# Two steps of small products interleaved on TensorE, with orders chosen anew, in a seven-attention transformer kernel

## The chip, the cores and the metric

One core of a Trainium2 chip runs the whole program. The metric is the time of one execution on the device in microseconds (us), as the median of the runs. PE is TensorE, DVE VectorE, ACT ScalarE, POOL GpSimd and SP SyncE.

## The reference

Four samples of 256 tokens with 128 features go through four blocks: ten sublayers in all. Seven are attention with 16 heads of 8 features, three are MLPs of 512 hidden features. What is computed, cut down:

```python
# x [4, 256, 128], cond [4, 128], ctx [4, 256, 128]
def attend(q, k, v, kind):                     # 16 heads of 8 features
    s = einsum('bhqd,bhkd->bhqk', q, k) / sqrt(8)
    if kind == 'window': # only keys of the same 64 tokens, tokens rolled by 32
        ...
    if kind == 'topk':   # softmax over the 16 largest scores of each query only
        top_s, top_i = top_k(s, 16)
        ...
    return einsum('bhqk,bhkd->bhqd', softmax(s), v)

# block 0: full self-attention, full cross-attention to ln(ctx), MLP (gelu)
# block 1: full self-attention, full cross-attention to ctx, MLP (gelu)
# block 2: full cross-attention to a modulated ln(ctx)
# block 3: window self-attention, top-16 cross-attention to ctx, MLP (swiglu)
x = x + gate * (attend(q(ln(x)), k(src), v(src), kind) @ w_o + b_o)
x = x + gate * (act(ln(x) @ w_up + b_up) @ w_down + b_down)
```

Layer norms are modulated by shifts and scales made from silu(cond).

## The kernel before

The program is a list of steps for each engine. A step is a tuple (kind, b, l, u): a kind of work, a sample b (0 to 3), a sublayer l and a part u. `plan` (lines 623 to 917) makes the lists before the program is emitted. It simulates the five engines with a table of durations (`BUSY`, line 147), takes whatever is ready, and where several steps are, the one with the highest rank: the length of the work behind it plus `LEAD` (per sample and sublayer), `BIAS` (per engine and kind) and `EXTRA` (per engine, kind, sample and sublayer). These three tables of numbers set the orders. The plan also hands out PSUM's eight banks (ring "bank"), the slots of the exponentials' buffer and others, and the emitted program waits on semaphores for what the plan says had them before. So each engine runs its list strictly in the order written.

For a full attention of one sample the steps are: PE makes queries and keys ("qk", lines 1517 and 1518); ACT and POOL split them in parts; four DMAs of POOL's queue bring them to the buffer `QKS` ("stack", line 1158), where each of four planes s holds four groups g of 32 rows, one head pair's operands in each. "scores" u = 0 to 7 (line 1536) multiplies groups 2(u%2) and 2(u%2)+1 of plane u//2, for both halves t of the queries: four matmuls of 32 rows and 256 columns into two banks. DVE takes the maxima of each step (line 1406). PE transposes the maxima, ACT copies them and a DMA of SP's queue writes them into row 31 of each group ("maxima"). "weights" u = 0 to 7 (line 1566) is the transposed product in the same form, on the same groups of rows; ACT makes the exponential of it (line 1298). "mix" (line 1590) multiplies with the values, then come the division, the output projection and the addition to x.

The window attention does eight smaller matmuls in each of four scores steps, and four in each weights step. In the top-k attention a step "topk" u = 0 to 15 (line 1544) makes one head's scores on the one group u%4 into one bank; DVE finds and strikes out the 8 largest twice (lines 1416, 1419, 1426, 1429), POOL makes a mask of what is left (line 1227), and PE adds it to the weights by eight more matmuls (line 1577).

The planner knows that steps on different groups of rows overlap on PE: `groups` (line 815) gives a step's groups as bits, and `beside` (line 822) says that a step starts right behind one that shares no group with it. Such a step gets 10 more in its rank (`BESIDE`) and costs 0.22 us less (with 0.2 us until its result is there). Scores and full weights steps cost 0.46 us, topk steps 0.4 us. Where PE would be idle for over 0.3 us, the plan puts spare matmuls on the identity (`SPARE`, line 1473).

In the emitter for PE a step's matmuls stand together. For scores:

```python
for i, s in enumerate(planes_of_scores(l, u)):
    pe.wait_ge(stacked[b][s], 16 * (l + 1))
    for t in range(NT):
        ...
        for j in range(2):
            g = 2 * (u % 2) + j
            ins = nc.tensor.matmul(...)
ins.then_inc(fin, 1)
```

## Time and profile before

| | us |
|---|---|
| median of 3 runs | 670.6 |
| lowest and highest of them | 669.71 and 672.51 |
| the profiled execution | 665.29 |
| its span, first to last instruction | 663.5 |
| PE busy | 570.0 |
| DVE busy | 490.9 |
| ACT busy | 386.3 |
| POOL busy | 306.4 |

The mean granted clock of PE was 0.863 of its full speed. Busy times are unions over the span; matmuls are pipelined, and a matmul's length in the trace includes time in which the next ones already run, so what a step costs PE is read from the start of the next one. PEld is the load of a matmul's stationary operand. "idle before" and "<-" give the idle time of the engine ahead of an instruction, and what ended it. L1536 is line 1536 of the kernel.

### The profile page before, as it was taken

To read this page: it belongs to the slowest core of one execution; us is meant where nothing else is said; L and a number is where in the kernel's file an instruction comes from. 1 tells how busy PE (TensorE), PEld (TensorE's weight loads), DVE (VectorE), ACT (ScalarE), POOL (GpSimd) and SP (SyncE) were. 2 spreads that over 40 slices of the span, in tenths; PEclk is the share of its full clock that TensorE was granted. 3 is DMA by queue.
4 is the path that set the end of the run, shared out by engine and by line. 5 is a ranking of instruction groups with operands and counts; after the bars stand their busy time and mean duration, and the time that the engine had idled before them with its cause. 6 is when DMAs were issued, how large, how long until landed. Compare 5 with 4: busy or idle time off the path is not lost.

```text
span 663.5 us, 14489 instructions
## 1 busy us (share of the span) xinstructions
PE 570.0 (86%) x5152; PEld 378.9 (57%) x5152; DVE 490.9 (74%) x1291; ACT 386.3 (58%) x669; POOL 306.4 (46%) x584
## 2 busy tenths in 40 slices
PE   3888989899999999999998889786999987867477
PEld 3645556566756565657665556554655664634246
DVE  2577767853859687745377727999999999999953
ACT  2546878799696887886757766452233531611133
POOL 6884535435845444364562446641341446111133
PEclk9858999999999999998989979777575795765779
DMA  9560344302333533020335043140020002000000
GB/s 319 143 159 3 88 106 112 73 2 54 76 67 69 105 77 78 2 65 2 66 72 123 2 129 68 28 101 0 2 65 2 2 10 64 9 1 2 1 2 16
DMA packets 15062, 39.23 MB, mean 59 GB/s; under 512 B 2641, under 2 KB 6801, under 8 KB 14737
## 3 DMA queue, kind: packets, MB, share of 16 engines
q0 software_dynamic: 8960, 29.37, 20.1%
q1 hardware_dynamic: 5312, 8.46, 3.8%
q8 instruction: 43, 0.70, 0.4%
q10 hardware_dynamic: 720, 0.49, 0.3%
q14 instruction: 27, 0.21, 0.1%
HBM read 7.96 MB, written 0.52 MB: 13 GB/s over the span
## 4 chain that ended last, share of the span: by engine, by line
DVE 38%; PE 37%; ACT 8%; DMA 6%; issue 6%; POOL 4%; ACTq 0%; POOLq 0%
PE psum L1590 10%; DVE left L1419 8%; DVE left L1429 7%; DVE top L1426 6%; DVE top L1416 6%; DVE maxima L1406 5%; PE psum L1566 5%; PE psum L1536 5%; ACT softmax_T L1298 4%; DMA qk_stack<-centred 3%; PE psum L1625 3%; PE psum L1636 3%; DMA qk_stack<-qk_parts 2%; DVE maxima L1402 2%; PE psum L1617 2%
## 5 line engine op out<-in xcount | busy, mean ns | idle before, releaser
L1298 ACT ACTIVATE softmax_T<-psum 128x1024 f32<-128x1024 f32 (+1 forms) x224 | 210.9, 962 | 111.7 <-PE psum L1577 73.3
L1406 DVE TENSOR_REDUCE maxima<-psum 128x4 f32<-128x1024 f32 x160 | 190.1, 1216 | 52.4 <-PE psum L1536 51.6
L1566 PE MATMUL psum<-qk_stack 32*128 32x256 f32 (+1 forms) x896 | 114.9, 346 | 28.1 <-DMA qk_stack<-centred 9.6
L1590 PE MATMUL psum<-softmax_T,values 128*32 128x256 f32 (+1 forms) x1792 | 129.9, 408 | 4.8 <-ACT softmax_T L1298 3.5
L1566 PEld LDWEIGHTS psum<-qk_stack 32*128 32x128 f32 x896 | 72.3, 202 | 71.0 <-issue 31.0
L1227 POOL TENSOR_SCALAR unpicked<-left 128x512 bf16<-128x512 f32 x64 | 39.5, 616 | 136.0 <-DVE left L1429 135.3
L1536 PE MATMUL psum<-qk_stack 32*128 32x256 f32 (+1 forms) x768 | 89.6, 335 | 9.2 <-ACT softmax_T L1298 2.4
L1536 PEld LDWEIGHTS psum<-qk_stack 32*128 32x128 f32 x768 | 58.9, 200 | 37.5 <-issue 16.5
L1590 PEld LDWEIGHTS psum<-softmax_T,values 128*32 128x32 f32 x1792 | 56.7, 118 | 40.3 <-issue 12.0
L1187 POOL TENSOR_TENSOR qk_parts<-qk_parts 128x256 fp32r<-128x256 f32 x56 | 40.9, 730 | 77.0 <-ACT qk_parts L1281 76.6
L1158 POOL DMA_DIRECT2D qk_stack<-qk_parts x112 | 63.7, 580 | 7.0 <-POOL qk_parts L1187 6.3
L1306 ACT ACTIVATE centred<-psum 8x256 f32<-8x256 f32 (+1 forms) x64 | 23.1, 364 | 56.3 <-PE psum L1551 40.9
L1278 ACT ACTIVATE qk_parts<-psum,column_biases 128x512 fp32r<-128x512 f32 x56 | 38.5, 687 | 24.0 <-PE psum L1518 21.0
L1419 DVE MATCH_REPLACE8 left<-top,psum 128x256 f32<-128x256 f32 x128 | 52.0, 414 | 0.0
L1429 DVE MATCH_REPLACE8 left<-top,left 128x256 f32<-128x256 f32 x128 | 51.4, 408 | 0.0
L1416 DVE MAX8 top<-psum 128x8 f32<-128x256 f32 x128 | 48.1, 417 | 2.0 <-PE psum L1544 2.0
L1426 DVE MAX8 top<-left 128x8 f32<-128x256 f32 x128 | 47.9, 416 | 1.3
L1448 DVE TENSOR_TENSOR x<-x,psum 128x256 f32<-128x256 f32 x40 | 16.6, 414 | 41.2 <-PE psum L1636 22.9
L1473 PE MATMUL psum<-identity 128*128 128x256 bf16 x150 | 27.4, 332 | 19.4 <-DVE left L1419 11.5
L1310 ACT ACTIVATE mixed_T<-psum 128x256 f32<-128x256 f32 x56 | 21.5, 385 | 31.9 <-PE psum L1590 31.3
L1172 POOL TENSOR_SCALAR centred<-x,neg_mean,rstd 128x128 f32<-128x128 f32 x80 | 35.2, 447 | 4.4
L1168 POOL TENSOR_SCALAR neg_mean<-mean_var 128x2 f32<-128x2 f32 x48 | 9.4, 196 | 58.6 <-DVE mean_var L1394 44.1
(99 smaller groups left out, 870.3 us busy)
## 6 DMA issues: line engine op xcount, KB each, us to landing
qk_stack<-qk_parts POOLq DMA_DIRECT2D x112, 256.0 KB, 5.1
weights<-in_w SPq DMA_DIRECT2D x1, 1408.0 KB, 13.5
row_biases<-in_rows SPq DMA_DIRECT2D x1, 1088.0 KB, 10.8
weights<-in_w SPq DMA_DIRECT2D x2, 512.0 KB, 5.9
weights<-in_w SPq DMA_DIRECT2D x1, 832.0 KB, 9.0
qk_stack<-centred SPq DMA_DIRECT2D x48, 8.0 KB
weights<-in_w SPq DMA_DIRECT2D x1, 768.0 KB, 4.3
weights<-in_w SPq DMA_DIRECT2D x1, 576.0 KB, 3.7
```

Of the source, the lines that this page charges most:

```text
L1158: pool.dma_start(QKS[b][:, u, :, :].bitcast(F32), parts[32 * u:32 * u + 32, slot, :, :, :].bitcast(F32)).then_inc(stacked[b][u], 16)
L1187: nc.gpsimd.tensor_tensor(lo, lo.bitcast(F32), parts[:, slot, 0, c, :].bitcast(F32), ALU.subtract).then_inc(done[kind, "pool"], 1)
L1227: nc.gpsimd.tensor_scalar(unpicked[:, n, :, :], left[:, k, :, :], 1.0 / GONE, 1.0, ALU.mult, ALU.add).then_inc(done[kind, "pool"], 1)
L1298: nc.scalar.activation(pT[:, slot, u % 2, :, 0:cols].rearrange("p (i t) n -> p i t n", t=NT), two_banks(step).rearrange("p i (t n) -> p i ...
L1406: nc.vector.tensor_reduce(rows[:, u // 4, u // 2 % 2, g:g + 2, :], ps.rearrange("p i (t k) -> p i t k", t=NT), AX_X, ALU.max).then_inc(fin, 1)
L1416: ins = nc.vector.max(top8[:, b, r, g, t, :], misc[:, N * t:N * t + N])
L1419: ins = nc.vector.match_replace(left[:, k, t, :], top8[:, b, r, g, t, :], misc[:, N * t:N * t + N], -GONE)
L1426: ins = nc.vector.max(top8[:, b, 2, g, t, :], left[:, k, t, :])
L1429: ins = nc.vector.match_replace(left[:, k, t, :], top8[:, b, 2, g, t, :], left[:, k, t, :], -GONE)
L1536: ins = nc.tensor.matmul(ps[:, j, at:at + (P if window else N)], QKS[b][32 * g:32 * g + 32, s, 0, P * t:P * t + P], QKS[b][32 * g:32 * g + ...
L1566: ins = nc.tensor.matmul(ps[:, i, t, 0:P if window else N], QKS[b][32 * g:32 * g + 32, s, 1, P * t:P * t + P], QKS[b][32 * g:32 * g + 32, ...
L1590: ins = nc.tensor.matmul(misc[32 * g:32 * g + 32, queries], V[:, b, t, first:first + 32], pT[:, slot, g // 2, 2 * (g % 2) + t, 0:P if wind ...
```

## The change

1. A step "weaves" if it is a full attention's scores, a topk step, or the weights of a full or window attention. When `plan` takes such a step for PE, it looks among PE's ready steps for another that weaves, on no common group, that can start within `TOGETHER` = 0.15 us. It takes the one with the highest rank, unless a step that doesn't fit has a rank higher by more than `BESIDE`. The two are planned as one piece of 0.50 us (0.40 behind a step beside the first), with the results at 0.46 and 0.52 us.
2. The emitter for PE waits for the banks and inputs of both steps and then issues half 0 of the first, half 0 of the second, half 1 of the first, half 1 of the second. A weaving step without partner is emitted as before.
3. In the plan an odd scores or weights step of a full attention (weights also of the window) no longer depends on the even one ahead of it, and scores of the window depend on both their planes' stacks.
4. The plan charges 0.62 instead of 1.0 us for POOL's stack step.
5. All of `EXTRA`, `BIAS` and `LEAD` are other numbers, so the orders of all engines, the slots and the spare matmuls are others.

```diff
-    ("pe", "qk"): 1.0, ... ("pool", "stack"): 1.0,
+    ("pe", "qk"): 1.0, ... ("pool", "stack"): 0.62,
...
+WOVEN, WOVEN_BESIDE, WOVEN_FIRST, WOVEN_SECOND, WOVEN_SLOWER, TOGETHER = 0.5, 0.1, 0.46, 0.52, 1.5, 0.15
...
+def weaves(step):
+    kind, b, l, u = step
+    if kind == "topk":
+        return True
+    return kind == "scores" and ATTN[l]["kind"] == "full" or kind == "weights" and ATTN[l]["kind"] != "topk"
...
-                    pe = task("pe", ("scores", b, l, u), stack[planes_of_scores(l, u)[-1]], t and ("pe", ("scores", b, l, u - 1)))
+                    pe = task("pe", ("scores", b, l, u), *[stack[s] for s in planes_of_scores(l, u)],
+                              ("pe", ("scores", b, l, u - 1)) if u and (u % 2 == 0 or lay["kind"] == "window") else None)
...
-                t = task("pe", ("weights", b, l, u), maxed[u // 2], prev and ("pe", ("weights", b, l, u - 1)),
+                t = task("pe", ("weights", b, l, u), maxed[u // 2], ("pe", ("weights", b, l, u - 1)) if u and (u % 2 == 0 or topk) else None,
...
+        if eng == "pe" and weaves(step):
+            others = [(rank(n), c[0], n) for n in ready["pe"] if (c := choose(n)) is not None]
+            fit = [o for o in others if weaves(o[2][1]) and not groups(o[2]) & groups(t) and o[1] <= s + TOGETHER]
+            if fit:
+                r, at, other = max(fit, key=lambda o: o[0])
+                if any(r + BESIDE < o[0] for o in others if o not in fit and o[1] <= s + 0.3):
+                    other = None
...
+        if other is not None:
+            s = max(s, at)
+            d = WOVEN - (WOVEN_BESIDE if beside(t, s) else 0.0)
+            last = groups(other)
+            end = clock.run(s, d, cells(step) + cells(other[1]), WOVEN_SLOWER)
+            ready["pe"].remove(other)
+            hold(other, choose(other)[1])
+            free["pe"] = end
+            woven[step] = other[1]
...
+            def inputs_in(step):
+                kind, b, l, u = step
+                if kind == "weights":
+                    pe.wait_ge(max_in[b], maxima_count(l, u // 2 if ATTN[l]["kind"] == "topk" else u // 4))
+                elif kind == "topk":
+                    pe.wait_ge(stacked[b][u // 4], 16 * (l + 1))
+                else:
+                    pe.wait_ge(stacked[b][u // 2], 16 * (l + 1))
+
+            def half(step, t):
+                kind, b, l, u = step
+                if kind == "topk":
+                    s, g = u // 4, u % 4
+                    return nc.tensor.matmul(bank(step)[:, N * t:N * t + N], QKS[b][32 * g:32 * g + 32, s, 0, P * t:P * t + P],
+                                            QKS[b][32 * g:32 * g + 32, s, 1, :], start=True, stop=True)
+                s, ps = u // 2, two_banks(step)
+                own, other = (1, 0) if kind == "weights" else (0, 1)
+                moving = slice(P * t, P * t + P) if ATTN[l]["kind"] == "window" else slice(0, N)
+                for j in range(2):
+                    g = 2 * (u % 2) + j
+                    ins = nc.tensor.matmul(ps[:, j, t * N:t * N + moving.stop - moving.start],
+                                           QKS[b][32 * g:32 * g + 32, s, own, P * t:P * t + P],
+                                           QKS[b][32 * g:32 * g + 32, s, other, moving], start=True, stop=True)
+                return ins
...
+                if weaves(step):
+                    inputs_in(step)
+                    if step in WOVEN_WITH:
+                        other = WOVEN_WITH[step]
+                        banks_free(pe, other)
+                        inputs_in(other)
+                        half(step, 0)
+                        half(other, 0)
+                        half(step, 1).then_inc(fin, 1)
+                        half(other, 1).then_inc(done[other[0], "pe"], 1)
+                    else:
+                        half(step, 0)
+                        half(step, 1).then_inc(fin, 1)
...
-LEAD = [[29.6, 27.3, 159.8, 27.1, 27.2, 25.2, 30.7, 27.0, 78.1, 420.1],
-        [18.3, 18.3, 18.3, 19.7, 18.7, -13.4, -10.7, -63.6, 338.4, -332.4],
-        [9.3, 9.1, 50.8, 7.5, 8.8, 525.5, 13.5, -500.4, -1.8, 224.2],
-        [1.3, 1.4, 437.2, -0.3, 0.9, -1.2, 4.4, 87.9, 52.7, -9.6]]
+LEAD = [[26.4, 26.8, 28.3, 27.1, 26.9, 28.9, 27.5, 21.7, 82.5, 1258.6],
+        [18.1, 18.0, 18.8, 18.2, 18.3, 19.5, 19.5, 9.1, -55.3, 769.2],
+        [8.9, 9.0, 35.6, 9.0, 9.2, 8.6, 8.3, -12.9, 633.7, 830.7],
+        [0.2, 0.0, 1.3, -1.4, 2.8, 187.4, 2.4, -3.5, -53.3, 404.5]]
```

## Rows read from the trace of the kernel before

**Rows 1.** The page, busy time (us), share of the span and instructions of each engine.

```profile
PE 570.0 (86%) x5152; PEld 378.9 (57%) x5152; DVE 490.9 (74%) x1291; ACT 386.3 (58%) x669; POOL 306.4 (46%) x584
```

**Rows 2.** Stretches: start:end, length, then busy us (instructions) per engine, clock, DMA share, GB/s.

```profile
50.00:400.00 350.00, 326.66 (x3368) 214.17 (x3366) 230.03 (x370) 271.37 (x459) 174.16 (x338) 0.97 0.29 65
250.00:300.00 50.00, 48.24 (x505) 31.08 (x506) 30.85 (x54) 41.94 (x67) 23.10 (x42) 1.00 0.20 45
450.00:600.00 150.00, 121.90 (x844) 80.43 (x842) 145.43 (x543) 51.01 (x84) 49.00 (x86) 0.68 0.08 17
400.00:664.00 264.00, 209.13 (x1577) 140.56 (x1577) 234.90 (x862) 94.57 (x167) 92.42 (x165) 0.74 0.10 23
```

**Rows 3.** Groups of DVE from 405 to 640 us: count | busy us, mean ns | idle.

```profile
L1419 DVE MATCH_REPLACE8 left<-top,psum 128x256 f32<-128x256 f32 x128 | 52.0, 414 | 0.0
L1429 DVE MATCH_REPLACE8 left<-top,left 128x256 f32<-128x256 f32 x128 | 51.4, 408 | 0.0
L1416 DVE MAX8 top<-psum 128x8 f32<-128x256 f32 x128 | 48.1, 417 | 2.0 <-PE psum L1544 2.0
L1426 DVE MAX8 top<-left 128x8 f32<-128x256 f32 x128 | 47.9, 416 | 1.3
```

**Rows 4.** Timeline of DVE: first and last search pass, last addition (start us, length us).

```profile
411.01 0.76 DVE L1416 MAX8 top<-psum 128x8 f32<-128x256 f32 x2 [1.95 <-PE psum L1544]
...
636.40 0.41 DVE L1429 MATCH_REPLACE8 left<-top,left 128x256 f32<-128x256 f32 x1
...
660.81 0.42 DVE L1448 TENSOR_TENSOR x<-x,psum 128x256 f32<-128x256 f32 x1 [1.77 <-PE psum L1636]
```

**Rows 5.** Timeline of PE's matmuls from 240 to 243 us, some of them.

```profile
240.03 0.38 PE L1536 MATMUL psum<-qk_stack 32*128 32x256 f32 x2
240.04 0.39 PE L1566 MATMUL psum<-qk_stack 32*128 32x256 f32 x2
240.25 0.28 PE L1536 MATMUL psum<-qk_stack 32*128 32x256 f32 x2
240.26 0.28 PE L1566 MATMUL psum<-qk_stack 32*128 32x256 f32 x2
240.47 0.71 PE L1523 MATMUL psum<-weights,context_T 128*128 128x128 f32 x4
...
242.66 0.50 PE L1536 MATMUL psum<-qk_stack 32*128 32x256 f32 x4
243.09 0.38 PE L1617 MATMUL psum<-gated_projection,normed_T 128*128 128x128 f32 x1
```

**Rows 6.** Timeline of PE, first and last of the 99 adjacent pairs.

```profile
28.94 1.56 PE L1536 MATMUL psum<-qk_stack 32*128 32x256 f32 x10 [1.42 <-ACT context_T L1248]
...
383.45 0.51 PE L1566 MATMUL psum<-qk_stack 32*128 32x128 f32 x8
```

**Rows 7.** Timeline of PE, two pairs whose steps start apart.

```profile
119.68 0.50 PE L1566 MATMUL psum<-qk_stack 32*128 32x256 f32 x4
120.18 0.51 PE L1536 MATMUL psum<-qk_stack 32*128 32x256 f32 x4
...
257.82 0.38 PE L1536 MATMUL psum<-qk_stack 32*128 32x256 f32 x2
257.99 0.38 PE L1566 MATMUL psum<-qk_stack 32*128 32x256 f32 x2
258.05 0.28 PE L1536 MATMUL psum<-qk_stack 32*128 32x256 f32 x2
...
258.42 0.33 PE L1605 MATMUL psum<-identity,centred 128*128 128x128 f32 x1
```

**Rows 8.** Groups by shape over the span: exponential and maximum.

```profile
L1298 ACT ACTIVATE softmax_T<-psum 128x1024 f32<-128x1024 f32 x192 | 192.6, 1021 | 100.5 <-PE psum L1577 73.3 <-PE psum L1566 25.5
L1406 DVE TENSOR_REDUCE maxima<-psum 128x4 f32<-128x1024 f32 x160 | 190.1, 1216 | 52.4 <-PE psum L1536 51.6
```

**Rows 9.** Groups by shape over the span: POOL's issue of a stack.

```profile
L1158 POOL DMA_DIRECT2D qk_stack<-qk_parts x112 | 63.7, 580 | 7.0 <-POOL qk_parts L1187 6.3 <-issue 0.4
```

More of the change, by code:

```diff
@@ L782, in plan @@
     lists = {e: [] for e in engines}
-    clock, spare = Clock(), {}
+    clock, spare, woven = Clock(), {}, {}
     table, last, queue = "exp", 0, 16.0
@@ L871, in plan @@
         d, lag = busy(t), 0.0
+        since = max([free["pe"], IDENTITY_THERE] + [when for _, which in taken for when, _, _ in which])
+        hold(t, taken)
+        other = None
[5 more added lines that the diff above has]
+                if any(r + BESIDE < o[0] for o in others if o not in fit and o[1] <= s + 0.3):
+                    other = None
+        if eng == "pe" and taken and s - since >= IDLE:
+            clock.until(since)
+            spare[step] = int(min(0.85 * (s - since), 0.3 + 0.6 * (s - since)) * (1.0 if clock.rate == 1 else 1 / 1.8) / SPARE_D)
+            if spare[step]:
+                clock.run(since, spare[step] * SPARE_D, spare[step] * SPARE_CELLS, 1.8)
+        if other is not None:
[7 more added lines that the diff above has]
+            woven[step] = other[1]
+            for n, land in ((t, WOVEN_FIRST), (other, WOVEN_SECOND)):
+                land = s + (end - s) / d * land
+                done[n] = (s, land)
+                lists["pe"].append(n[1])
+                landing(n, land, end)
+            left -= 2
+            continue
         if beside(t, s):
```

498 lines of the change are left out of this document (234 added, 264 removed), and 324 rows, old and new, of the table EXTRA.

## The prediction

> **What bounds the kernel now.** I read the page's busy shares first. PE is busy for 86% of the span, DVE for 74% and ACT for 58% [rows 1], but these are means over stages with different limits, so the table by stretches comes next. The reader is to see two stages in it. Between 50 and 400 us PE is busy for 326.7 of 350 us at a granted clock of 0.97 on the mean, with 48.2 of 50 in the fullest stretch, while DVE has 66% and ACT 78%: PE sets the pace. Between 450 and 600 us DVE is busy for 145.4 of 150 us, and PE's clock is down to 0.68 without anybody missing it [rows 2]. What fills DVE there are the four passes of the top-k search, 52.0 + 51.4 + 48.1 + 47.9 = 199.4 us [rows 3]. The first pass starts at 411.0 and the last ends at 636.8; behind it there is a tail of single instructions that wait for each other, which ends with the down product and its addition [rows 4].
>
> So the span is: a stage of some 411 us that PE bounds, 225.8 us bound by DVE, and a tail of 26.7 us. The search work is the same before and after. Time can be won where PE is the bound, and it is passed on only if the search then starts earlier.
>
> **What a step costs on PE.** A step of full scores or weights is four matmuls of 32 rows and 256 columns, two for each half t. Alone it holds PE for 0.43 us: the scores step that begins at 242.66 is followed by the residual product at 243.09 [rows 5]. Within a step the second half starts 0.22 us after the first (240.03 and 240.25), since it loads other weights into the same rows.
>
> **The interleaving itself.** The change issues half 0 of step A, half 0 of step B, half 1 of A, half 1 of B, where the kernel before issued all of A and then all of B. The trace of before already shows the order that this asks for. At 240.03 a scores step and at 240.04 a weights step start their first halves, their second halves follow at 240.25 and 240.26, and the next step starts at 240.47 [rows 5]: two steps in 0.44 us, though the program has A's second half ahead of B's first. So for a pair that is adjacent and ready the interleaving is worth 0. I laid the list of PE's steps, in its order, beside the matmuls of the timeline, and counted. Ahead of 405 us there are 99 adjacent pairs of steps that may be interleaved and lie on different row groups (the first and the last are in [rows 6]). By how long after A's start B starts, they are: 34 within 0.07 us, 25 at 0.07 to 0.25 (as at 257.82 and 257.99, where the next step starts at 258.42, which is 0.43 after B), 18 at 0.25 to 0.43, and 22 later, at 0.80 us on average (as the one at 119.68 and 120.18). These two cases are in [rows 7]. In the last three groups B was not ready, and an interleaved pair begins when both are: PE is done at the same time, and A alone is later, by those delays. The direct effect is therefore nothing on PE and at most a small loss for A's reader.
>
> The Trainium skill, TensorE: Matmul & The Clock Gate, section "Part 3: Packing small matmuls", says that only weight loads are pulled ahead and that matmuls keep strict program order. By that rule B's first half could not pass A's second, and interleaving by hand would bring each ready pair from two steps in a row to one. The rows at 240.03 to 240.26 speak against it.
>
> **The added wait.** In a pair PE now waits for B's banks and inputs before A's first matmul. Behind that wait stands all of PE's queue, mixes and projections too, and behind A its reader (DVE's maximum, 1.22 us, or ACT's exponential, 1.02 us [rows 8]). If the plan is right, both are ready within 0.15 us (TOGETHER), and it costs 0 to 0.15 us; if it is wrong, it costs what the pairs above show, 0.17 us (257.82 to 257.99) up to 0.80 us. I take 0, by the 34 pairs that started together, and keep the other end for the range.
>
> **The new orders.** This is what can move the time. The planner used to charge a pair 0.46 + 0.24 us and now charges 0.50 us, or 0.40 behind another step beside it. Of the weavable steps ahead of 405 us, 99 pairs hold 198 and 130 are alone, so 60% are paired. Each further pair takes one single step's 0.43 us off PE. I suppose that orders chosen with the cheaper pair, and with a dependence of odd steps on their even neighbours taken away, pair three quarters: 246 of 328 steps, 123 pairs, 24 more, 24 x 0.43 = 10.3 us. The ends are 0 (the shares stay as they are) and all of them, 65 x 0.43 = 28 us. The quarter is my choice: PSUM has eight banks, a pair takes four, and scores are asked to leave three free, so pairs of two scores steps stay rare.
>
> Not all of 10.3 us arrives. ACT is busy for 271.4 us of the 350 [rows 2]; it waits for weights products for 25.5 us and DVE for scores for 51.6 us in all [rows 8], so both have room for a PE that is quicker by 10 in 355, but the transfers of maxima and of the stacked queries and keys in each sample's chain don't shrink. PE is busy for 93% of the stage (326.7 of 350); I round that down to 0.8 for those chains and take 8.3 us; the ends are 0 and 1.
>
> The spare matmuls on the identity are placed anew in gaps, worth 0: they stand where PE would be idle, and if a gap were gone they would cost what they last. The stack step's charge on POOL falls from 1.0 to 0.62 us; its DMA issue lasts 0.58 us in the trace [rows 9], so the plan gets truer. POOL is busy for 46% [rows 1] and I put that at 0. The searches, the top-k weights (not interleaved), window scores and the tail are as before: 0, if the order keeps DVE as dense as now. Top-k steps may be interleaved too, but DVE needs 2 x (0.417 + 0.414 + 0.416 + 0.408) = 3.3 us for what PE makes in one step [rows 3], so 0.
>
> **The sum.** The profiled execution took 665.3 us, 663.5 of it the span. 665.3 - 8.3 = 657.0 us. The median of the runs is 670.6, which is 5.3 above the profiled one, so on the median's scale 670.6 - 8.3 = 662.3 us.
>
> **Rivals.**
> 1. *No more pairs.* The new orders pair as many steps as the old, the hardware overlapped those already, and the time stays at 670.6 (668 to 673). For it: 0.44 us for a pair at 240.03. Against it: 130 steps alone leave room.
> 2. *Slower: a pair waits for its later half.* The plan's readiness is not the chip's: 65 of the 99 pairs started more than 0.07 us apart although they were planned next to each other. If 120 pairs begin on average 0.15 us late, and PE stands, that is 18 us against the 10.3 of fewer steps: 8 us slower, 678.5. It decides from 10.3 / 120 = 0.09 us a pair on. Against it: a late B held PE in the old order as well, only A went ahead.
> 3. *Strict order.* If PE kept its matmuls in program order but for cases like 240.03, interleaving would also save the half step of 0.22 us in the 43 pairs that started 0.07 to 0.43 us apart, 9.5 us: 670.6 - 8.3 - 9.5 = 652.8. The rows at 257.82 speak against it: B's first half (257.99) starts ahead of A's second (258.05) there too [rows 7]. The rule of the Trainium skill that is named above is of this kind.
> 4. *Better orders beyond pairs.* PE was idle for 23 us between 50 and 400 (350 less 326.7 [rows 2]), and a plan that knows when a pair ends could fill a part: another 6 to 8 us, about 655.
>
> **Chances.** The forecast 0.40 (own range 656 to 668), rivals 3 and 4 together 0.15 (0.05 and 0.10), rival 1 0.20, rival 2 0.25. What a measurement of this kernel can tell from no change is 0.5%, 3.4 us. Faster 0.55, same 0.20, slower 0.25. The range leaves out the far halves of rivals 2 and 4 and what lies beyond 28 us of pairs: 650 to 678.
>
> **What would show it.** Right: in the stage up to the first search, fewer lone steps (some 82 where there were 130), pairs at 0.44 us, PE's busy time for the two products lower, and the first search pass some 8 us earlier with DVE still as dense behind it (145 of 150 us). Rival 1: the first search where it was. Rival 2: PE idle ahead of pairs, released by ACT, DVE or the maxima's DMA, for over 10 us more than before. Rival 3: pairs at 0.44 us where the kernel before with the same adjacency has 0.65. The prediction is wrong at its root if the new orders leave gaps in DVE's stage, since none of the sums above hold there.

## The result, and the profile after

| | before | after |
|---|---|---|
| median of 4 runs, us | 671.56 | 685.99 |
| lowest and highest | 669.71 and 673.53 | 679.62 and 687.61 |
| the profiled execution | 665.29 | 687.61 |
| its span | 663.5 | 685.8 |

The changed kernel is slower: the ratio is 1.0197, with a 95% interval of 1.0121 to 1.0273, which lies clear of 1 and on both sides of 1.02. Ratios and intervals are of the fast executions alone, those within 1.5% of the fastest of their kernel, while medians are of all. The forecast was 662.3 us, in a range of 650 to 678. The profiled execution of before lies 6 us under its median and that of after 2 us above its own, so of the 22.3 us between the two profiles some 14 are the change and the rest is scatter. Another profile of the same kernel after, in a later comparison (681.81 us, ratio 1.019), had a span of 678.1. I name both where the size matters.

First the page of after: busy time, share and instructions of each engine. It answers to [rows 1].

```profile
PE 582.6 (85%) x5166; PEld 382.5 (56%) x5166; DVE 492.5 (72%) x1291; ACT 382.7 (56%) x667; POOL 306.4 (45%) x583
```

The work is the same: the 1291 instructions of DVE are all there, POOL's time is equal, and PE is busy for 12.6 us more in a span that is 22.3 longer. Next the stretches of after, with the columns of [rows 2] (start:end, length, busy us (instructions) of PE, PEld, DVE, ACT and POOL, clock, DMA share, GB/s).

```profile
50.00:400.00 350.00, 323.56 (x3316) 207.03 (x3314) 227.20 (x367) 269.04 (x455) 169.07 (x327) 0.93 0.27 60
450.00:600.00 150.00, 120.07 (x868) 77.59 (x871) 143.15 (x544) 47.55 (x78) 46.60 (x81) 0.65 0.10 23
413.70:436.50 22.80, 22.09 (x182) 15.95 (x178) 11.46 (x18) 8.48 (x20) 7.98 (x16) 0.50 0.33 79
```

In the stage that PE bounds, the clock is 0.93 on the mean where it was 0.97, and in the fullest stretch of before, 250 to 300 us, PE is busy for 46.0 of 50 us (48.2 before). DVE's stage is as dense as it was: 143.2 of 150 us against 145.4. The last row is the time from sample 0's window-attention addition to the first search: all of it at the lower level of the clock. The same way took 14.0 us in the kernel before (397.0 to 411.0), at a clock of 1.00.

Then the timeline of DVE (start us, length us), which answers to [rows 4]: the first search pass, the last, and the last addition.

```profile
436.49 0.76 DVE L1434 MAX8 top<-psum 128x8 f32<-128x256 f32 x2
...
658.55 0.41 DVE L1447 MATCH_REPLACE8 left<-top,left 128x256 f32<-128x256 f32 x1
...
683.15 0.42 DVE L1466 TENSOR_TENSOR x<-x,psum 128x256 f32<-128x256 f32 x1 [2.15 <-PE psum L1681]
```

The three parts of the span are now 436.5, 222.5 and 24.6 us up to the last addition; they were 411.0, 225.8 and 24.4. The search and the tail together are 3.1 us shorter. All the time is lost ahead of the first search, which starts 25.5 us later (in the other profile of after at 426.7, 15.7 us later).

More of the work stands ahead of the first search than before: 3793 of PE's matmuls are recorded up to it where there were 3700, and 451 of DVE's instructions where there were 443. The lists of the two plans say which: four scores steps, two weights steps, two mixes and one whole attention's addition to x more, and four more spare matmuls. At the mean of 92.5 ns a matmul that PE has in b_spares (below), these 90 are some 8 us of PE's time, an estimate, which the stage behind gets back in part.

**What PE does there.** These are the groups of PE's matmuls on stacked queries and keys from 50 us to the first search (count, busy us as a union, mean ns, idle time ahead of them by its releaser), first of before, where scores and weights have a line each, then of after, where the woven ones share a line. The window scores of after have a line of their own, with 13.5 us and 0.8 us of idle time.

```profile
L1566 PE MATMUL psum<-qk_stack 32*128 32x256 f32 (+1 forms) x680 | 80.2, 327 | 7.9 <-DMA qk_stack<-centred 4.7 <-ACT softmax_T L1298 1.6 <-DVE maxima L1406 0.6
L1536 PE MATMUL psum<-qk_stack 32*128 32x256 f32 (+1 forms) x678 | 75.5, 321 | 6.5 <-ACT softmax_T L1298 2.4 <-DMA qk_stack<-qk_parts 2.0 <-DVE maxima L1406 1.1
```

```profile
L1505 PE MATMUL psum<-qk_stack 32*128 32x256 f32 (+1 forms) x1268 | 114.8, 342 | 22.3 <-DMA qk_stack<-centred 7.3 <-ACT softmax_T L1316 7.0 <-DVE maxima L1424 5.7
```

PE is idle ahead of the products for 23.1 us instead of 14.4, and most of the growth is behind readers that have to free a bank: ACT's exponential and DVE's maxima released 5.7 us of that idle time before and 12.7 after. The experiments below show that this part comes with the interleaving and not with the new orders. And the rest is slower: a matmul of the mix takes 415 ns on the mean instead of 388, at the lower clock.

The busy times of the two lines of before can't be added up, since scores and weights steps run at the same time ([rows 5]) and their sum counts that time twice. What the products hold PE for is the union over all of them. Here it is (stretch, length, busy us (matmuls), clock, DMA share, GB/s) for before and after, and then for b_spares and a_spares, which are the same two with spare matmuls in the gaps (below) and have nearly the same clock:

```profile
50.00:411.00 361.00, 127.63 (x1361) 0.97 0.29 65
50.00:436.50 386.50, 127.58 (x1400) 0.91 0.29 64
50.00:412.80 362.80, 124.92 (x1368) 0.99 0.29 66
50.00:426.00 376.00, 117.62 (x1396) 0.98 0.29 65
```

In the first two the time is equal, for 39 matmuls more and at a lower clock. In the last two it falls by 7.3 us for 28 matmuls more: from 91 to 84 ns for each, which for 1396 of them is 10 us. Without the interleaving (a_unwoven_spares) it is 120.6 us for 1398, 86 ns each, and the saving 7 us. So the saving by more pairs is there, and about as large as the prediction had it; by these profiles the interleaving itself adds some 3 us to it.

**Pairs.** Laying the list of PE's steps beside its matmuls, as in the prediction, gives 141 adjacent pairs on different rows in the whole program where there were 118 (81 of the 141 are interleaved), and 134 steps alone where there were 180. Ahead of the planned first search it is 121 pairs where there were 100, and 98 steps alone where there were 136. One interleaved pair, and two groups of the window attention near the end of the stage, in the timeline of PE after:

```profile
237.91 0.51 PE L1505 MATMUL psum<-qk_stack 32*128 32x256 f32 x8 [0.43 <-ACT softmax_T L1316]
238.34 0.71 PE L1662 MATMUL psum<-gated_projection,normed_T 128*128 128x128 f32 x4
238.99 1.09 PE L1635 MATMUL psum<-softmax_T,values 128*32 128x256 f32 x16
...
411.40 0.69 PE L1505 MATMUL psum<-qk_stack 32*128 32x128 f32 x8 [2.46 <-DMA qk_stack<-centred]
412.02 1.22 PE L1662 MATMUL psum<-gated_projection,normed_T 128*128 128x128 f32 x4
413.18 0.69 PE L1505 MATMUL psum<-qk_stack 32*128 32x128 f32 x8
```

Two steps (8 matmuls) hold PE for 0.43 us, and so does one step (4 matmuls, 242.23 to 242.66). The four matmuls of L1662 hold it for 0.65 us at 238.34 (2.4 GHz) and for 1.16 us at 412.02 (1.2 GHz): what a stretch at the lower level costs is read from such pairs.

### The profile page after: what moved, and what is told of

The parts are those of the page before. It is cut to its first block, busy times and chain, and to the rows that moved or that the text cites. A ratio compares the mean times of both kernels' runs of the same rounds, so it can differ in the third digit from the quotient of the medians.

```text
span 685.8 us, 14510 instructions
## 1 busy us (share of the span) xinstructions
PE 582.6 (85%) x5166; PEld 382.5 (56%) x5166; DVE 492.5 (72%) x1291; ACT 382.7 (56%) x667; POOL 306.4 (45%) x583
## 4 chain that ended last, share of the span: by engine, by line
PE 42%; DVE 24%; ACT 11%; DMA 9%; issue 7%; POOL 5%; ACTq 0%; POOLq 0%
PE psum L1635 12%; PE psum L1505 10%; DMA qk_stack<-centred 7%; ACT softmax_T L1316 6%; DVE left L1437 5%; DVE left L1447 5%; DVE maxima L1424 4%; DVE top L1444 4%; DVE top L1434 4%; PE psum L1681 3%; DMA qk_stack<-qk_parts 2%; PE psum L1662 2%; PE psum L1521 2%; PE psum L1670 1%; PE psum L1578 1%
## 5 line engine op out<-in xcount | busy, mean ns | idle before, releaser
L1505 PE MATMUL psum<-qk_stack 32*128 32x256 f32 (+1 forms) x1408 | 135.3, 351 | 32.9 <-DMA qk_stack<-centred 10.2
L1635 PE MATMUL psum<-softmax_T,values 128*32 128x256 f32 (+1 forms) x1792 | 140.6, 437 | 3.0 <-ACT softmax_T L1316 1.7
L1505 PEld LDWEIGHTS psum<-qk_stack 32*128 32x128 f32 x1408 | 88.8, 207 | 96.0 <-issue 45.8
L1635 PEld LDWEIGHTS psum<-softmax_T,values 128*32 128x32 f32 x1792 | 60.3, 125 | 43.3 <-issue 20.1
L1466 DVE TENSOR_TENSOR x<-x,psum 128x256 f32<-128x256 f32 x40 | 16.6, 416 | 43.2 <-PE psum L1662 30.6
L1521 PE MATMUL psum<-identity 128*128 128x256 bf16 x164 | 33.6, 362 | 14.2 <-DVE cond_silu L1364 7.0
L1615 PE MATMUL psum<-qk_stack 32*128 32x256 f32 x128 | 21.1, 417 | 20.7 <-ACT softmax_T L1316 7.8
L1420 DVE TENSOR_REDUCE maxima<-psum 128x8 f32<-128x1024 f32 x16 | 19.4, 1223 | 22.9 <-PE psum L1595 22.9
L1188 POOL TENSOR_TENSOR rstd<-var_eps,half_power 128x2 f32<-128x2 f32 x48 | 33.9, 707 | 4.0
## 6 DMA issues: line engine op xcount, KB each, us to landing
row_biases<-in_rows SPq DMA_DIRECT2D x1, 1088.0 KB, 10.8
```

The source lines that it names most:

```text
L1505: ins = nc.tensor.matmul(ps[:, j, t * N:t * N + moving.stop - moving.start], QKS[b][32 * g:32 * g + 32, s, own, P * t:P * t + P], QKS[b][3 ...
L1521: nc.tensor.matmul(psum[:, SLOT["bank", step][0], 0:2 * P], ident[:].bitcast(BF16)[:, 0:P], ident[:].bitcast(BF16), start=True, stop=True)
L1635: ins = nc.tensor.matmul(misc[32 * g:32 * g + 32, queries], V[:, b, t, first:first + 32], pT[:, slot, g // 2, 2 * (g % 2) + t, 0:P if wind ...
```

## The kernel's own plan beside the chip

The plan is made from charges, and its times can be laid beside the trace: both know when sample 0's addition of a sublayer ends and when the first search starts. The difference, chip minus plan, is called the lag here. Sublayers are counted from 0 in the order of the network, so that 7 is the window attention.

| kernel | addition 1 | 3 | 6 | first search: plan, chip, lag | end: plan, last addition on the chip, lag |
|---|---|---|---|---|---|
| before | 4.9 | 3.2 | 3.7 | 401.8, 411.0, 9.2 | 650.4, 661.2, 10.8 |
| after | 9.8 | 11.1 | 19.5 | 403.1, 436.5, 33.4 | 646.3, 683.6, 37.3 |
| after, other profile | 4.7 | 7.4 | 15.8 | 403.1, 426.7, 23.6 | 646.3, 675.8, 29.5 |

The end of a plan is its last store, 0.8 us behind its last addition, so the lags at the end are 0.8 us too small, all by the same.

The new orders promised 4.1 us less in all, and nothing for the first search (403.1 against 401.8), though in their plan a pair is charged 0.50 us or 0.40 and not 0.70. The chip follows the old plan at a distance of 1 to 6 us until sublayer 6 and falls behind the new one throughout. From sublayer 6 to the first search the lag grows in both, by 5.5 us before and by 13.9 and 7.8 after.

## Experiments

Each run is compared with runs of the kernel before on the same chip, which had medians of 669.35 to 672.31 us. Single executions of it lay between 660.53 and 678.46 us, so a ratio is given with its interval, and differences of a few tenths of a per cent rest on little.

### The interleaving alone

Runs a_unwoven and a_unwoven_again keep all orders of after and emit each step as before. Runs b_woven and b_woven_again keep all orders of before and interleave the 73 adjacent pairs whose second step the plan has ready in time. Runs b_waits and b_order take b_woven apart.

```diff
 # a_unwoven, on after
-                if step in WOVEN_WITH.values():
-                    continue
...
-                    if step in WOVEN_WITH:
+                    if False and step in WOVEN_WITH:
 # b_woven, on before: half() and the branch of after, and pairs found in the old list
+    if (weaves(_a) and weaves(_b) and not rows_of(_a) & rows_of(_b) and not SPARE.get(_b)
+            and there(_b) <= TIMES["pe", _a][0] + 0.15):
+        WOVEN_WITH[_a] = _b
 # b_waits: the waits of both first, the halves in the old order
 # b_order: the halves interleaved, the second step's waits behind the first's half 0
```

> The changed kernel with its new orders, slots and spare matmuls, but each step emitted by itself as before: the 81 interleaved pairs are issued as all of A, then B's waits, then all of B. Theory 1 (the loss is in the new orders, the interleaving itself is worth 0): 1.02 times the kernel before, 681 to 688 us, two ready steps still in 0.44 us. Theory 2 (pairs that wait for their later half cost the time): 0.99 to 1.00 times the kernel before, since A no longer waits for B. Theory 3 (interleaving saves a half step of 0.22 us a pair): slower than the changed kernel by up to 81 x 0.22 = 18 us, over 1.04.

> The same kernel as a_unwoven. If the interleaving costs time of its own (0.5% between the first two measurements), the ratio to the changed kernel of this call is 0.990 to 0.996; if it is worth nothing, 0.998 to 1.002.

> The kernel before with its own orders, slots and spare matmuls; 73 of its 118 adjacent pairs, those that the plan has ready within 0.15 us of each other, are interleaved as in the change (waits of both first, then half 0 of A, half 0 of B, half 1 of A, half 1 of B). Theory 1 (interleaving worth 0): 0.995 to 1.005. Theory 2 (the wait for the later half costs 0.1 to 0.2 us a pair): 1.01 to 1.02. Theory 3 (interleaving saves 0.22 us a pair that isn't tight): 0.98 to 0.99.

> The same kernel as b_woven, in more runs: the first four gave 1.0095, and moving only the waits or only B's waits gave 0.996 both, which one cause can't give. If interleaving costs of its own: 1.006 to 1.012 again. If the first figure was scatter: 0.997 to 1.004.

> As b_woven (the kernel before's orders, 73 pairs), but only the waits are moved: PE waits for both steps' banks and inputs, then issues all of A and then all of B. If the later half's wait is what cost b_woven its 0.95%: 1.006 to 1.012, as b_woven. If the interleaved issue is: 0.997 to 1.003.

> As b_woven, but B's waits stand behind A's first half: wait for A, half 0 of A, wait for B, half 0 of B, half 1 of A, half 1 of B. If waiting for the later half is the cost, A is still held up, now with half of it done: 1.005 to 1.012. If only the start of A ahead of B's readiness matters: 0.998 to 1.004.

| run | median us (runs) | ratio to before |
|---|---|---|
| a_unwoven | 679.05 (4) | 1.0142 [1.0066, 1.0217] |
| a_unwoven_again | 681.84 (6) | 1.0156 [1.0059, 1.0253] |
| after_again (below), beside a_unwoven_again on the same chip | 681.81 (6) | 1.0190 [1.0081, 1.0299] |
| b_woven | 675.82 (4) | 1.0095 [1.0016, 1.0174] |
| b_woven_again | 673.44 (12) | 1.0069 [1.0001, 1.0136] |
| b_waits | 671.98 (10) | 0.9964 [0.9907, 1.0020] |
| b_order | 671.86 (10) | 0.9964 [0.9917, 1.0010] |

On the new orders the interleaving makes no difference that can be measured: 681.84 without it and 681.81 with it on the same chip, 1.0142 and 1.0156 against 1.0197 and 1.0190 as ratios. So at least 1.4% are there without it, and a cost of its own of some 0.5% isn't excluded by the intervals. The first run came out at 679.05 us, a little under the 681 to 688 that theory 1 had. A pair that isn't interleaved, in the timeline of PE of a_unwoven:

```profile
244.22 0.52 PE L1505 MATMUL psum<-qk_stack 32*128 32x256 f32 x8
244.66 0.39 PE L1603 MATMUL psum<-identity,maxima 128*8 128x128 f32 x2
```

It holds PE for 0.44 us, as the interleaved one does for 0.43. So most of the slowdown lies in the orders. On the old orders the interleaving costs 0.7 to 0.9%, twice at the edge of the scatter; in the second of these runs the medians of all executions, 673.44 and 671.89 us, differ by 0.2% only. Its two parts by themselves, the waits moved ahead and the halves interleaved, cost nothing. I can't say what makes them cost something together, or whether they do; the cause stays open.

The traces say a little more. Here are the products' groups of a_unwoven and of b_woven, to be laid beside those of after and before:

```profile
L1505 PE MATMUL psum<-qk_stack 32*128 32x256 f32 (+1 forms) x1264 | 117.9, 338 | 16.1 <-DMA qk_stack<-centred 9.5 <-ACT softmax_T L1316 2.6 <-DVE maxima L1424 2.3
L1520 PE MATMUL psum<-qk_stack 32*128 32x256 f32 (+1 forms) x1240 | 118.2, 330 | 14.6 <-ACT softmax_T L1331 4.0 <-DVE maxima L1439 3.9 <-DMA qk_stack<-centred 2.8
```

On the new orders the two readers released 12.7 us with the interleaving and 4.9 without it, which is less than in the kernel before. Summed over all of PE's waits up to the first search, the tiles of the exponential and the maxima released 10.9 us before, 13.7 in b_woven and 16.4 in b_waits, and 18.0 and 17.2 in the two profiles of after against 9.9 and 10.5 without interleaving. So these waits come with the waits moved ahead, and they don't decide the time: b_waits is no slower, and a_unwoven_again is as slow as after. Sample 0's addition of the window attention ends at 397.0 us before, at 401.8 and 402.4 in the two profiles with interleaving, at 413.7 and 411.2 after and at 404.5 and 406.6 without interleaving. In both sets of orders the interleaved profiles are some 5 to 9 us behind there. On the new orders nothing of it is left at the first search beside after_again (426.7, against 426.8 and 426.9 without), because the way from that addition to the search ran at a clock of 0.50 and 0.65 in the profiles without interleaving and at 1.00 in after_again.

### The kernel after once more

> The changed kernel once more, to have it on one chip and in more runs beside the two below. 1.015 to 1.024.

It took 681.81 us, ratio 1.0190 [1.0081, 1.0299]: the result repeats. Its profile has the first search at 426.7 and not 436.5, and it is the one with the smaller lags in the table above. So a part of the 25.5 us in the first pair of profiles is the draw of one execution; 15.7 is the other value. Most of the 9.8 us between them lie on sample 0's way from its window addition to the first search: 22.8 us in the first profile and 15.5 in this one, by the same program. Here is that way in after_again and in a_spot (the next section), to be laid beside the last of the stretches of after above:

```profile
411.20:426.70 15.50, 13.60 (x186) 9.59 (x181) 11.21 (x17) 7.83 (x19) 9.86 (x20) 1.00 0.58 118
417.00:432.70 15.70, 14.31 (x193) 10.36 (x193) 11.20 (x17) 7.94 (x20) 8.21 (x17) 1.00 0.50 109
```

At a granted clock of 1.00 the way takes 15.4 to 15.7 us in four profiles of the new orders (a_spares 15.6 and a_unwoven_spares 15.4 are the others), and at 0.50 it takes 22.3 us (a_unwoven) and 22.8. So of the 8.8 us by which it is longer in the first profile of after than before, 7.3 are the clock and 1.5 the changed kernel.

### Is it the clock? Spare matmuls in every gap

The spare matmuls on the identity keep PE busy where it would be idle. I added 188 of them to after and 131 to before, at the steps ahead of which the trace showed over 0.2 us of idle time; a_unwoven_spares has those of after without interleaving, and a_spot has only 26, ahead of four steps between 408 and 420 us, where the clock of after fell.

```diff
+MORE = {('scores', 1, 0, 3): 4, ('weights', 0, 0, 4): 2, ..., ('weights', 1, 5, 0): 16, ...}
+for _s, _n in MORE.items():
+    SPARE[_s] = SPARE.get(_s, 0) + _n
```

> The changed kernel with 188 more spare matmuls on the identity, put at the 55 steps between 45 and 436 us before which PE stood idle for over 0.2 us in its trace (1 to 24 each, about 0.11 us apiece for seven tenths of the gap). Clock theory (the changed kernel spends 47 us of the stretch from 50 to 400 us at the lower clock where the kernel before spends 24, and that costs about 10 us): the cold time there falls under 20 us and the time by 6 to 12 us, to 1.00 to 1.01. If the clock is not a cause: the same cold time or no gain, 1.015 to 1.03.

> The kernel before with 131 more spare matmuls at the 38 steps between 45 and 411 us before which PE stood idle for over 0.2 us in its trace. Clock theory: the cold time from 50 to 400 us falls from 24 us to under 12, and the time by 2 to 5 us, 0.992 to 0.998. If spare matmuls only take PE's time: 1.00 to 1.01.

> The changed kernel's orders with both undone: each step emitted by itself, and the 188 more spare matmuls of a_spares. If interleaving (0.5%) and the clock (0.7%) are separate causes, their gains add up: 1.004 to 1.010, and what is left over 1.000 is the orders' own. If they are the same cause (the waits make the gaps that lower the clock): 1.011 to 1.014, as either alone.

> The changed kernel with 26 more spare matmuls only, at the four steps between 408 and 420 us before which PE stood idle (3, 16, 3 and 4). The clock fell at 411.3 us there and stayed down for 72 us, while sample 0's way from its last window addition (413.7) to its first search (436.5) took 22.8 us against 14.0 in the kernel before. Clock theory: that way shrinks to 15 to 18 us and the time by 4 to 8 us against the changed kernel, 1.008 to 1.014. If the orders alone make it long: 22 us again and 1.018 to 1.022.

| run | median us (runs) | ratio to before | first search |
|---|---|---|---|
| a_spares | 677.33 (4) | 1.0125 [1.0064, 1.0187] | 426.0 |
| b_spares | 668.73 (4) | 1.0004 [0.9934, 1.0075] | 412.8 |
| a_unwoven_spares | 679.89 (4) | 1.0123 [1.0038, 1.0208] | 423.6 |
| a_spot | 684.09 (4) | 1.0143 [1.0050, 1.0235] | 432.7 |

The clock theory had a_spares at 1.00 to 1.01 and b_spares at 0.992 to 0.998; both missed it. The result of a_unwoven_spares, 1.0123, is the one expected if the gains by the clock and by undoing the interleaving don't add up. In a_spot the way from the window addition to the search shrank to 15.7 us, as the clock theory had it (15 to 18), and its time, 1.0143, is at the edge of the 1.008 to 1.014 expected with it.

Here are the stretches of a_spares and of b_spares from 50 us to their first searches, and the group of the spare matmuls in each (count, busy us, mean ns, idle time ahead).

```profile
50.00:426.00 376.00, 353.78 (x3782) 231.72 (x3780) 244.50 (x392) 285.12 (x493) 186.06 (x358) 0.98 0.29 65
L1524 PE MATMUL psum<-identity 128*128 128x256 bf16 x188 | 31.2, 285 | 11.7 <-ACT softmax_T L1319 6.4 <-DVE maxima L1427 3.7 <-ACT normed_T L1279 0.5
```

```profile
50.00:412.80 362.80, 345.47 (x3636) 227.65 (x3630) 238.73 (x383) 281.49 (x481) 183.67 (x355) 0.99 0.29 66
L1476 PE MATMUL psum<-identity 128*128 128x256 bf16 x126 | 20.7, 280 | 9.9 <-ACT softmax_T L1301 6.0 <-DVE maxima L1409 2.1 <-ACT qk_parts L1284 1.4
```

This pair is the fairest comparison of the orders, since the clock is nearly the same in both. Without the spare matmuls PE works for 353.8 - 31.2 = 322.6 us in a_spares and 345.5 - 20.7 = 324.8 us in b_spares. That is 2.2 us less, for 3594 matmuls instead of 3510: what the pairs save is spent on the work that the new orders put ahead of the search. And PE has nothing of its own to do for 376.0 - 322.6 = 53.4 us against 362.8 - 324.8 = 38.0 us: 15.4 us more. Without the interleaving, in a_unwoven_spares, it works for 355.5 - 30.9 = 324.6 us up to 423.6 and has nothing of its own for 373.6 - 324.6 = 49.0 us, 11.0 more than b_spares. So 11.0 us of the 15.4 are there without the interleaving.

What PE waits for in them isn't settled by this. The readers released 11.0 us of idle time in a_unwoven_spares and 10.1 in b_spares, so banks held by these readers don't explain it. The spare matmuls are issued behind a step's wait for its banks and cover part of its wait for inputs. They may themselves hold steps up, and not evenly: 10.5 of the 15.4 us are spare matmuls' own time, of which a_spares has 188 in the stretch and b_spares 126.

The clock adds to it. Full of spare matmuls, the new orders gain 0.7% with interleaving (1.0197 to 1.0125; the first search at 426.0 and not 436.5) and 0.2 to 0.3% without it (1.0142 and 1.0156 to 1.0123), and the old ones gain nothing. All these intervals overlap. In a_spot the first search stands at 432.7, in the longest of its four executions (689.44 us); the window addition was already at 417.0 there. So of the 2%, some 0.2 to 0.7 is the clock, which is lower in the new orders where their gaps aren't filled (0.93 and 0.95 from 50 to 400 us, 0.99 with the spare matmuls). The remaining 1.2% is there at a clock of 0.98 up to the first search, with the interleaving or without it.

### Is it a charge? The stack step alone

The old kernel with its own tables, and only the stack's charge as in after.

```diff
-    ... ("pool", "stack"): 1.0,
+    ... ("pool", "stack"): 0.62,
```

> The kernel before with one number of its plan changed, the charge for POOL's stack step, 0.62 in place of 1.0 us, as in the change; its tables are kept. The plan made with it ends at 690.3 us where the kernel before's own ends at 650.4: tables that were chosen for one set of charges don't suit another. If the plan follows the chip as it does for the kernel before (chip's last addition 10.8 us behind the plan), the time is 700 to 708 us. If the new plan's lag of 37 us (683.6 against 646.3) is of any plan, 725 to 735.

It took 722.89 us in two runs, ratio 1.0848 [1.0730, 1.0966], which lies between the two times expected (700 to 708 and 725 to 735). Most of this is the plan itself: with one charge changed the same ranks give other lists, whose end is planned at 690.3. Its plan and the chip stand at 436.9 and 456.9 for the first search (lag 20.0) and at 690.3 and 720.2 for the end (lag 29.9), three times the lag of before. But up to sublayer 6 it is 5.4 us, close to the 3.7 of before: this lag arises behind that, in part on the way from the window addition to the search, which took 25.7 us at a clock of 0.50.

The issue of a stack lasts 0.58 us as the prediction said. In the trace the time from the first of four issues to the landing of the fourth has a median of 7.78 us before and 7.80 us after, where the old charges plan 8.5 us and the new ones 8.1. So the new charge is truer and even still on the safe side. It takes 0.38 us out of each attention's chain in the plan.

### Is it luck? Other orders from both planners

A list of orders is one draw, and a planner with a simulated end that is just as good could have drawn a better or worse one. I walked `EXTRA` at random, keeping the plan's end: two draws from the planner of before (259 and 222 of PE's 896 adjacencies are others) and two from that of after (282 and 302).

```diff
-    ("act", "context", 0, 0): 7.6, ("act", "context", 0, 3): 8.7, ...
+    other numbers in EXTRA, nothing else
```

> The kernel before with other numbers in EXTRA, found by small random steps that left its plan's end at 650.4 us (planned before: 650.4) but changed 259 of PE's 896 adjacencies. Luck theory (the lag of the chip behind a plan differs by 10 us and more from plan to plan, and the kernel before has an early one): 675 to 690 us. Slack theory (the old plan charges an adjacent pair 0.70 us where the chip takes 0.44, so that chips keep up with any such plan): 667 to 674 us.

> As walk_old1, by other random steps: plan's end 650.5 us, 222 adjacencies of PE's list changed. Luck theory 675 to 690 us, slack theory 667 to 674 us.

> The old planner's walk with the plan's end at 650.5 us once more. If its 0.989 of the first time is its own, the ratio is 0.985 to 0.995 again; if it was the scatter of runs, 0.995 to 1.005. By the theory of slack (same charges as the kernel before, same planned end) it lies within 0.5% of the kernel before, with a lag of 6 to 15 us; by the rival, that orders are luck, it may lie anywhere from 0.985 to 1.02.

> The changed kernel with other numbers in EXTRA, found the same way: plan's end 647.1 us (the changed kernel's 646.3), 282 adjacencies changed. Luck theory: anywhere from 670 to 695 us. Slack theory (the new plan charges a pair 0.50 us, which leaves the chip nothing to catch up with): 680 to 690 us, as the changed kernel.

> The kernel after, with other numbers in EXTRA (a second random walk): its planner's end is 647.6 us, that of the kernel after is 646.3, and 302 of 896 adjacencies of PE's steps are others. Theory (a plan whose charges leave no slack is run late by the chip): 680 to 700 us, a ratio of 1.013 to 1.04 to the kernel before, the last addition 30 to 45 us later than planned. Rival (the orders of the kernel after are one unlucky draw): the plan is at least as good as that of the kernel before (650.4), so 665 to 675 us, and a lag of 8 to 20 us as there.

| run | planned end | median us (runs) | ratio to before | lag at first search | lag at end |
|---|---|---|---|---|---|
| walk_old1 | 650.4 | 674.98 (9) | 1.0067 [0.9985, 1.0149] | 8.5 | 16.6 |
| walk_old2 | 650.5 | 669.89 (3) | 0.9887 [0.9748, 1.0027] | 0.6 | 6.3 |
| walk_old2_again | 650.5 | 667.68 (12) | 0.9976 [0.9944, 1.0009] | 3.9 | 12.6 |
| walk_new1 | 647.1 | 694.95 (3) | 1.0291 [1.0192, 1.0390] | 36.1 | 43.7 |
| walk_new3 | 647.6 | 691.36 (4) | 1.0320 [1.0261, 1.0380] | 32.1 | 41.8 |

Of the expectations, walk_old2 and walk_new3 are within what the theory of reserve (slack) says; walk_old1, with 674.98 us, is just above its 667 to 674, where the luck theory begins (675), and walk_new1 is 5 us above its 680 to 690.

Up to sublayer 6 the lag is 4.7 us in walk_old1 and 1.1 in walk_old2_again, and 27.5 in walk_new1 and 18.6 in walk_new3.

The orders of after are not an unlucky draw near their own: they are the best of three lists from that planner, which share two thirds of their adjacencies. The three sets from the old planner run at 0.998 to 1.007, with lags of 6 to 17 us at the end, and the three from the new one at 1.019 to 1.032, with lags of 30 to 44, although each plan of the new planner ends 3 to 4 us earlier. The 0.989 of walk_old2 was scatter: 0.998 in 12 runs. No version beats the kernel before by what can be measured.

### Is it the new ranks? The new planner with the old ranks

The kernel after with the three tables of before and the stack's charge at 1.0, which leaves the cheaper pair, the freed dependences and the interleaving.

```diff
-    ... ("pool", "stack"): 0.62,
+    ... ("pool", "stack"): 1.0,
-EXTRA, BIAS, LEAD of after
+EXTRA, BIAS, LEAD of before
```

> The change's planner and emitter with the old tables and the old charge for POOL's stack step: its plan ends at 680.3 us, against 650.4 for the kernel before. The chip's last addition was 10.8 us behind the plan in the kernel before, 37 in the changed kernel and about 30 in old_stack062 (plan 690.3). If the lag belongs to the planner that weaves: 37 behind again, some 720 us. If it is of most plans: 705 to 725.

The ranks don't fit this planner (its end is planned at 680.3), and only two runs compare, 728.56 and 829.28 us, so no ratio is given. The time is near the 720 us expected if the lag belongs to the new planner. The profile can be read against its own plan: the first search at 460.4 where 425.3 was planned, a lag of 35.1, and 44.2 at the end (724.5 against 680.3). So the lag comes with the new planner even where the stack's charge is the old one. At sublayer 6 it is 28.3 us here and 5.4 in old_stack062. In the stage that PE bounds, the lag therefore goes with what the new planner and its emitter have left in this run, the cheaper pair, the freed dependences and the interleaving, and not with the stack's charge. The interleaving's part can be told for after: without it the lag at sublayer 6 is 10.3 and 11.2 us (a_unwoven, a_unwoven_again) instead of 19.5 and 15.8. No run here divides the other two, and each change of one draws new orders.

## Why the prediction was wrong, by its own steps

- **What bounds the kernel**: right. The search stage and the tail changed by 3.1 us together, and all the rest is in the stage ahead of the first search. DVE's stage stayed dense, so what the text called its root held.
- **A pair and a step alone take 0.44 and 0.43 us**: right (0.43, 0.44 and 0.43 in the rows above).
- **The interleaving itself is worth 0**: right on the new orders within the scatter (681.81 and 681.84 us). The forecast for rival 3, pairs at 0.65 us where the kernel isn't interleaved, is refuted by the 0.44 us at 244.22, and so is, for this kernel, the rule that it came from: the Trainium skill, TensorE: Matmul & The Clock Gate, section "Part 3: Packing small matmuls", has matmuls in strict program order, while the second halves and first halves on different rows pass each other in [rows 5].
- **The added wait costs 0**: not shown to be wrong by any time on the new orders. It isn't nothing in the traces: the readers released 7.8 us more of PE's idle time with the interleaving. On the old orders interleaving cost 0.7 to 0.9%, which is within the range that the prediction kept (up to 18 us), but the waits alone cost nothing (0.9964).
- **24 more pairs, 10.3 us**: right. Ahead of the planned first search 100 became 121, 21 more (23 in the whole program), though 98 steps stayed alone where the prediction had some 82. At nearly equal clock they are worth 7 us without the interleaving and 10 with it, by 91, 86 and 84 ns a product matmul.
- **0.8 of the 10.3 us arrives**: this step failed; none of it arrived. The factor had no measured source (0.93 rounded down to 0.8), and 0.8 x 10.3 is 8.2 and not 8.3. The first search came 15.7 or 25.5 us later and not 8 earlier. The pairs' saving was real, but from 50 us to the first search PE's own work fell by 2.2 us only (324.8 to 322.6 at nearly equal clock), since the new orders put some 90 more matmuls ahead of it. The prediction took the work ahead of the search as given. Its argument that ACT and DVE "both have room for a PE that is quicker by 10 in 355" isn't what failed: the waits for these two readers ahead of the products rose from 5.7 to 12.7 us with the interleaving, but without it they are 4.9 and the kernel is as slow.
- **The new orders are as good as the old otherwise, and a plan that "gets truer" is worth 0**: this is the deeper error, and it had no term and no rival. The new plan promised the first search at 403.1 where the old one had it at 401.8: the planner itself saw no gain of 8.3 us there, and this could have been read before the change was timed. And the chip didn't keep it. At nearly equal clock PE has nothing of its own to do for 15.4 us more up to the search (53.4 for 38.0), 11.0 of them without the interleaving. Up to sublayer 6 the chip stays within 6 us of the old plan and is 15.8 or 19.5 us behind the new one (10.3 and 11.2 without the interleaving). The old charges were too high by 0.70 - 0.44 = 0.26 us a pair and by some 0.7 us a stack of four (8.5 planned, 7.78 measured). That the chip follows plans with such a reserve in the pair's charge and falls behind plans without it fits the lags, three lists of each planner and new_oldtables, and is argued: the freed dependences changed with it, and why PE waits longer in the new orders stays open. For the stack's charge the lag of 5.4 us at sublayer 6 in old_stack062 speaks against it. It isn't excluded either that the old planner's walks run well because the orders of before happen to suit the chip, since they keep some three quarters of its adjacencies.
- **The clock**: no term. The prediction took PE's lower clock as a matter of the search stage, where nobody misses it. The gaps of the new orders brought it into the stage where PE is the bound: 0.93 and 0.95 for 0.97 between 50 and 400 us, and in one of two profiles 0.50 for the 22.8 us ahead of the first search, which take 15.5 at 1.00. By the spare matmuls it is worth 0.2 to 0.7% of the time.
- **Rival 2** had the sign and 678.5 us, but its mechanism explains only a small part: it wanted interleaved pairs that wait for their later half, and 1.4 to 1.6% are there without any interleaving. Its sign in the profile, over 10 us more idle time ahead of pairs, came out at 8.7 us (14.4 to 23.1), and it is the interleaving that brings it: 16.7 without. A rival for orders that are worse in themselves was missing, as were its chance and its price.

## What to carry to other kernels

When a change replaces the whole order of a kernel, forecast the order and not only the edit: read what the new plan promises against the old one, and how far the chip ran behind the old plan, and give "these orders run worse" a chance and a price of its own. A charge in a static plan that is longer than what the trace shows may be a reserve against what the plan doesn't know; here the plans without it were 3 to 4 us shorter and the runs 2 to 3% longer. Count the work ahead of the step that starts the next stage in both lists: what a change saves can be spent there. And before a growing wait is called the cause, undo the part of the change that makes it: here it went away and the time stayed.

## What was not expected of the hardware

A gap of 2.46 us on PE (408.95 to 411.40, while it waited for the DMA of the maxima) stands right ahead of a stretch in which the granted clock is 0.50 for 22.8 us, although PE is busy for 22.09 us of it. The same program had that way at 1.00 in another execution, and took 15.5 us for it. PE's matmuls on different rows overlap fully across a step's boundary: 8 of them in the 0.43 or 0.44 us of 4, interleaved in the program (237.91) or not (244.22, [rows 5]). The third is the scatter: executions of one and the same kernel before lay between 660.5 and 678.5 us over all comparisons, more than most of the effects here.
